# Grams as two 64-row products in two banks, a ring of three ScalarE banks, X0 by two 78-row transposes

## The reference

```python
e = stack([tbl_f[ids[:, f]] for f in range(39)], axis=1)          # 512 x 39 x 16
def _cin_layer(X0, Xi, W, b):
    Wr = W.reshape(H, F0_, Fi)
    return einsum('hjk,bjd,bkd->bhd', Wr, X0, Xi) + b[None, :, None]
Xi = X0 = e
for W, b in ((W0, b0), (W1, b1), (W2, b2)):                         # H = 128
    Xi = _cin_layer(X0, Xi, W, b); res.append(Xi.sum(axis=2))
z = concatenate(res, axis=1)                                        # 512 x 384
h = maximum(concatenate([z, dense_ctx], axis=1) @ W_top1 + b_top1, 0)
y = maximum(h @ W_top2 + b_top2, 0) @ W_top3
```

## Time and profile before

| | us |
|---|---|
| median of 3 timed runs | 656.97 (655.59 to 658.33) |
| the profiled execution | 650.86 |
| its span, first to last instruction | 649.1 |
| PE busy | 616.1 |
| DVE busy | 579.1 |
| ACT busy | 557.4 |
| POOL busy | 467.5 |

### The profile page before, as it was taken

The page is one execution under the profiler, slowest core; times in us unless marked ns, Lnnn a source line. Parts: engine busy times, 40 slices in busy tenths (PEclk is TensorE's granted clock), DMA queues, the critical chain, the costliest instruction groups (busy, mean ns, idle before and its releaser), DMA issues.

```text
span 649.1 us, 14322 instructions
## 1 busy us (share of the span) xinstructions
PE 616.1 (95%) x2591; PEld 477.4 (74%) x2591; DVE 579.1 (89%) x1230; ACT 557.4 (86%) x1763; POOL 467.5 (72%) x437
## 2 busy tenths in 40 slices
PE   0399999999999999999999999999999999999998
PEld 0167787878878787878787887878787878776573
DVE  0578999999999999999999999999999999999780
ACT  2177999999999999999999999999999999998572
POOL 6779988889797979898798979797987666220000
DMA  8543405050413223140405041322314050000100
GB/s 223 145 108 72 124 9 144 11 139 20 115 45 93 66 66 94 31 129 7 137 18 141 18 121 38 94 65 65 95 36 122 6 149 2 12 2 17 66 1 0
DMA packets 44274, 46.16 MB, mean 71 GB/s; under 512 B 20896, under 2 KB 27264, under 8 KB 44233
## 3 DMA queue, kind: packets, MB, share of 16 engines
q1 hardware_dynamic: 38626, 43.59, 23.7%
q0 software_dynamic: 5120, 1.32, 2.3%
q10 hardware_dynamic: 487, 0.74, 0.4%
HBM read 44.30 MB, written 1.31 MB: 70 GB/s over the span
## 4 chain that ended last, share of the span: by engine, by line
PE 86%; DVE 5%; DMA 3%; issue 3%; SPq 1%; DVEq 1%; ACT 1%; ACTq 0%
PE ya L513 12%; PE ya L514 12%; PE ya L515 12%; PE yd L513 9%; PE yd L515 8%; PE yd L514 8%; PE misc L496 5%; PE acc L485 4%; PE acc L484 4%; PE acc L486 3%; DVE chain L636 2%; DMA w<-in_w 2%; PE acc L489 1%; DMA tiles<-x_rows 1%; PE yd L587 1%
## 5 line engine op out<-in xcount | busy, mean ns | idle before, releaser
L764 ACT ACTIVATE prods<-ya,x0t 128x128 f32<-128x128 f32 x1472 | 453.3, 511 | 37.2 <-PE ya L515 36.5
L636 DVE SCALAR_TENSOR_TENSOR chain<-yd,x0t,chain 128x128 f32<-128x128 f32 x768 | 218.4, 343 | 1.8 <-PE yd L515 1.6
L391 POOL DMA_INDIRECT emb<-in_tables,rows x160 | 157.4, 984 | 35.6 <-issue 24.9
L513 PE MATMUL ya<-w1h,x1h 128*128 128x512 f32 (+1 forms) x384 | 166.5, 434 | 1.1 <-DVE x1l L704 1.1
L426 POOL TENSOR_TENSOR prod0l<-prod,prod0h 120x512 fp32r<-120x512 f32 x98 | 127.7, 1303 | 48.5 <-ACT prod0h L773 47.6
L514 PE MATMUL ya<-w1l,x1h 128*128 128x512 f32 (+1 forms) x384 | 147.6, 384 | 0.0
L515 PE MATMUL ya<-w1h,x1l 128*128 128x512 f32 (+1 forms) x384 | 147.4, 384 | 0.0
L305 POOL TENSOR_TENSOR prod<-tiles,x0a 120x512 f32<-120x512 f32 x105 | 137.1, 1306 | 8.6 <-DMA tiles<-x_rows 3.3
L651 DVE TENSOR_REDUCE x2t<-prods 128x128 f32<-128x1792 f32 x64 | 129.2, 2019 | 2.4 <-DVE chain L636 0.3
L651 DVE TENSOR_REDUCE prods<-prods 128x128 f32<-128x1536 f32 x64 | 111.8, 1746 | 0.0
L513 PE MATMUL yd<-w1h,x1h 128*128 128x512 f32 x256 | 102.4, 400 | 2.6 <-DVE prods L636 2.2
(11 more groups left out here) (99 smaller groups left out, 610.0 us busy)
## 6 DMA issues: line engine op xcount, KB each, us to landing
tiles<-x_rows SPq DMA_DIRECT2D x236, 78.0 KB
x0a<-x_rows SPq DMA_DIRECT2D x45, 80.0 KB
emb<-in_tables,rows POOLq DMA_INDIRECT x160
w<-in_w SPq DMA_DIRECT2D x3, 832.0 KB, 11.0
w<-in_w SPq DMA_DIRECT2D x13, 192.0 KB, 2.4
tiles<-x_rows SPq DMA_DIRECT2D x32, 42.0 KB
x<-x_rows SPq DMA_DIRECT2D x16, 78.0 KB
x<-x_rows SPq DMA_DIRECT2D x16, 77.8 KB
```

Of the source, the lines that this page charges most:

```text
L391: pool.indirect_dma_start(emb[:, c % 2, fo * D:(fo + 1) * D], None, a["tables"], bass.IndirectOffsetOnAxis(ap=rows[:, c, fo:fo + 1].bitcas ...
L513: pe.matmul(out, x1h[:, c % 2, xs], w1h[:, cols], start=True, stop=False)
L636: dve.scalar_tensor_tensor(out, product, x, run if step else b1[:, :], ALU.mult, ALU.add).then_inc(yd_used, 1)
L764: mm = act.activation(prods[:, :, slot_of(q) + i], ya[(NA * g + k) % YA][:, i * H:(i + 1) * H], ACT.Copy, scale=turned(c)[:, g * F1 + j:g ...
```

## The change

Four things change together.

1. A gram becomes two products of 64 rows. The two halves of a group's partitions now hold 4 samples each (`HB`), so the diagonal has 4 x 40 = 160 columns for both, and the mask repeats every 4 rows. Rows 0 to 63 go into bank `pair[:, 0]`, rows 64 to 127 into `pair[:, 1]`. ACT's copy reads both banks in one instruction. `misc` is the first bank of `pair`.
2. For the second bank the ring of ScalarE's banks shrinks from four to three (`YA`). In the tail the last hidden product takes `pair[:, 1]`.
3. Within a chunk all columns of the first half of the samples come before those of the second, group by group 64 and 64. So the rows in DRAM are stored as two halves of 256 columns, and each load and store addresses half rows: 1 KB pieces where there were 2 KB, and 64 bytes in the store where there were 128.
4. `x0` holds two copies (`XB = 2`), loaded by two DMAs in place of three, and two transposes of 78 rows turn it.

```diff
+HB = GB // 2
+HROWS = P // 2
+HCOLS = COLS // 2
-XB = 3
+XB = 2
-YA, YD = 4, 2
+YA, YD = 3, 2
+DIAGS = 2
-        diag = sb("diag", [P, 2, GB, F1])
+        diag = sb("diag", [P, DIAGS, HB, F1])
-        scratch = nc.dram_tensor("x0_rows", (CHUNKS, FP, COLS), F32, kind="Internal").ap()
-        acc0, misc = ps("acc0"), ps("misc")
+        scratch = nc.dram_tensor("x0_rows", (CHUNKS, 2, FP, HCOLS), F32, kind="Internal").ap()
+        acc0, pair = ps("acc0"), ps("pair", (P, 2, 512))
+        misc = pair[:, 0, :]
 def load_x0a(engine, x):
-                engine.dma_start(x0a[u * R0:(u + 1) * R0, :], chunk_rows(x)[0:R0, :]).then_inc(x0a_in, 16)
+                engine.dma_start(in_halves(x0a[u * R0:(u + 1) * R0, :]), chunk_rows(x)[0:R0]).then_inc(x0a_in, 16)
 def load_x0(x):
-                    sp.dma_start(x0[g * F:(g + 1) * F, 0:COLS - g], chunk_rows(x)[0:F, g:COLS]).then_inc(x0_in, 16)
+                    sp.dma_start(in_halves(x0[g * F:(g + 1) * F, :])[:, :, 0:HCOLS - g], chunk_rows(x)[0:F, :, g:HCOLS]).then_inc(x0_in, 16)
 def block_diagonal(c, g):
-                mask = const[:, C_MASK:C_MASK + GB].rearrange("p (b o) -> p b o", o=1)
-                pool.tensor_tensor(diag[:, n % 2, :, :], row.to_broadcast([P, GB, F1]),
-                                   mask.to_broadcast([P, GB, F1]), ALU.mult).then_inc(diag_ready, 1)
+                mask = const[:, C_MASK:C_MASK + HB].rearrange("p (b o) -> p b o", o=1)
+                pool.tensor_tensor(diag[:, n % DIAGS, :, :], row.to_broadcast([P, HB, F1]),
+                                   mask.to_broadcast([P, HB, F1]), ALU.mult).then_inc(diag_ready, 1)
 def turn_x0(c):
                 pe.transpose(misc[:, 0:XB * F], by_group[:, 0, :], const[0:XB * F, C_ID:C_ID + XB * F])
-                pe.transpose(misc[:, XB * F:GROUPS * F], by_group[0:F, XB, :], const[0:F, C_ID:C_ID + F]
+                pe.transpose(misc[:, XB * F:2 * XB * F], by_group[:, XB, :], const[0:XB * F, C_ID:C_ID + XB * F]
                              ).then_inc(x0t_done, 1)
 def gram_group(n, g):
-                pe.matmul(misc[:, 0:GB * F1], x2t[:, g % 2, :],
-                          diag[:, g % 2, :, :].rearrange("p b j -> p (b j)"),
-                          start=True, stop=True).then_inc(g_done, 1)
+                for h in range(2):
+                    half = slice(h * HROWS, (h + 1) * HROWS)
+                    mm = pe.matmul(pair[:, h, 0:HB * F1], x2t[half, g % 2, :],
+                                   diag[half, g % DIAGS, :, :].rearrange("p b j -> p (b j)"), start=True, stop=True)
+                mm.then_inc(g_done, 1)
 def evacuate_gram(n, i=0):
-                act.activation(gram[:, :, bass.ds(n * GB, GB)],
-                               misc[:, 0:GB * F1].rearrange("p (b j) -> p j b", b=GB),
+                cols = slice(i * HB * F1, (i + 1) * HB * F1)
+                act.activation(gram[:, :, bass.ds(n * GB, GB)].rearrange("p j (h b) -> p j h b", h=2),
+                               pair[:, :, cols].rearrange("p h (b j) -> p j h b", b=HB),
                                ACT.Copy).then_inc(g_ready, 1)
...
```

More of the change, by code:

```diff
@@ L54 @@
 C_MASK = 0
-C_ID = C_MASK + GB
+C_ID = C_MASK + HB
 C_ALL = C_ID + P
@@ L274, in chunk_rows, with in_halves @@
         def chunk_rows(c):
-            return scratch[bass.ds(c, 1), :, :].rearrange("c r n -> (c r) n")
+            return scratch[bass.ds(c, 1), :, :, :].rearrange("c h r n -> r (c h) n")
+        def in_halves(x):
+            return x.rearrange("p (h n) -> p h n", h=2)
         def turned(c):
@@ L293, in load_tile @@
             for row, a, b in segments(i):
-                engine.dma_start(tiles[a:b, i % L0_TILES, :],
-                                 chunk_rows(x)[row:row + b - a, :]).then_inc(tile_in[i % L0_TILES], 16)
+                engine.dma_start(in_halves(tiles[a:b, i % L0_TILES, :]),
+                                 chunk_rows(x)[row:row + b - a]).then_inc(tile_in[i % L0_TILES], 16)
         def multiply0(engine, x, i):
@@ L306, in multiply0 @@
                                  ALU.mult).then_inc(prod0_ready, 1)
-        hid, hid2 = (acc0, ya[0], ya[1], ya[2]), (yd[1], ya[3])
+        hid, hid2 = (acc0, ya[0], ya[1], ya[2]), (yd[1], pair[:, 1, :])
         block = ctx.enter_context(nc.Block())
@@ L316, in store_x0 @@
                 sp.wait_ge(x0_ready, x + 1)
[L317 to L320, removed]
+                by_row = scratch[x, :, :, :].rearrange("h (f o) n -> (h f) (o n)", f=FI)
+                for i, cols in enumerate((slice(0, FT * HCOLS), slice(FT * HCOLS, FO * HCOLS))):
+                    sp.dma_start(by_row[:, cols].rearrange("q (p b) -> p q b", b=CB // 2),
+                                 xt[0:(cols.stop - cols.start) // (CB // 2), i, :].rearrange("p (q b) -> p q b", b=CB // 2),
                                  ).then_inc(scratch_in, 16)
@@ L398, in block_diagonal @@
                 pool.wait_ge(x0t_ready, c + 1)
-                wait_done(pool, g_done, n - 1)
+                wait_done(pool, g_done, n - DIAGS + 1)
                 row = x0t[:, c % XT, g * F1:(g + 1) * F1].rearrange("p (o j) -> p o j", o=1)
-                mask = const[:, C_MASK:C_MASK + GB].rearrange("p (b o) -> p b o", o=1)
-                pool.tensor_tensor(diag[:, n % 2, :, :], row.to_broadcast([P, GB, F1]),
-                                   mask.to_broadcast([P, GB, F1]), ALU.mult).then_inc(diag_ready, 1)
+                mask = const[:, C_MASK:C_MASK + HB].rearrange("p (b o) -> p b o", o=1)
+                pool.tensor_tensor(diag[:, n % DIAGS, :, :], row.to_broadcast([P, HB, F1]),
+                                   mask.to_broadcast([P, HB, F1]), ALU.mult).then_inc(diag_ready, 1)
             def clear_dense():
@@ L664, in sum_dims @@
                     dve.wait_ge(l0_done, T0 + z_tiles)
-                dve.tensor_reduce(z[:, bass.ds(c * CB, CB)].rearrange("p (g b) -> p g b", g=GROUPS),
-                                  x1[:, :].rearrange("p (g d b) -> p g b d", g=GROUPS, d=D), AX.X,
+                dve.tensor_reduce(z[:, bass.ds(c * CB, CB)].rearrange("p (g b) -> p g b", g=2 * GROUPS),
+                                  x1[:, :].rearrange("p (g d b) -> p g b d", g=2 * GROUPS, d=D), AX.X,
                                   ALU.add).then_inc(z_sums, 1)
@@ L730, in evacuate_layout, with by_half @@
                 wait_done(act, scratch_in, 2 * 16 * c)
-                act.activation(xt[:, 0, :], misc[:, 0:P], ACT.Copy)
-                act.activation(xt[0:FO * D - P, 1, :], misc[0:FO * D - P, P:2 * P], ACT.Copy).then_inc(x0_ready, 1)
+                def by_half(x, order):
+                    return x.rearrange(f"p ({order} b) -> p f h b", h=2, b=CB // 2)
+                act.activation(by_half(xt[:, 0, :], "h f"), by_half(misc[:, 0:P], "f h"), ACT.Copy)
+                act.activation(by_half(xt[0:FO * D - P, 1, :], "h f"), by_half(misc[0:FO * D - P, P:2 * P], "f h"),
+                               ACT.Copy).then_inc(x0_ready, 1)
             def evacuate_x0t(c):
@@ L748, in evacuate_x1, with evacuate_gram @@
                                ACT.Copy).then_inc(x1h_ready, 1)
-            def evacuate_gram(n):
+            def evacuate_gram(n, i=0):
                 act.wait_ge(g_done, n + 1)
-                act.activation(gram[:, :, bass.ds(n * GB, GB)],
-                               misc[:, 0:GB * F1].rearrange("p (b j) -> p j b", b=GB),
+                cols = slice(i * HB * F1, (i + 1) * HB * F1)
+                act.activation(gram[:, :, bass.ds(n * GB, GB)].rearrange("p j (h b) -> p j h b", h=2),
+                               pair[:, :, cols].rearrange("p h (b j) -> p j h b", b=HB),
                                ACT.Copy).then_inc(g_ready, 1)
@@ L851, in constants @@
     for row in range(P):
-        pack[row, C_MASK + row % GB] = 1.0
+        pack[row, C_MASK + row % HB] = 1.0
         pack[row, C_ID + row] = 1.0
```

## The result

The changed kernel takes 661.13 us (median of 9 runs, 659.8 to 662.37), the kernel before 656.04 us beside it (9 runs, 653.18 to 659.38): ratio 1.0069, 95% interval 1.005 to 1.0087. It is slower by 0.7%, about 4.5 us by the ratio (the medians lie 5.1 us apart). The forecast was +16.2 us, 673.2 us: the right direction, more than three times the size. The time lies within the stated 658 to 686, near its lower end, and within 0.3 us of rival A's 661.4. The experiments show that A's sum is right by luck: two of its terms are wrong, and their errors cancel.

What follows compares the result with a forecast made beforehand. The prediction took PE to bound the loop, with DVE not far behind. Grams +20.1, transposes -5.1, banks +0.3 and DMA +0.9 gave +16.2 us on 656.97, so 673.2 us; range 658 to 686 for 8 in 10.

Steps and rivals of the forecast that it cites:

- rival A: Grams on PE: halves overlap fully but the emptying stays, 59 x 0.14 = +8.3 us, in all 661.4 us; chance 0.15.
- A nanosecond added to PE there is a nanosecond of the span.: Steady loop: PE, busy 36.00 of 36 us, is the bound, so time added to PE lengthens the span equally.
- Part 1, entering and leaving, 0.21 and 0.20: Each gram on PE: emptying costs 0.21 us before the 64-row passes and 0.20 us in the product behind.
- Part 1, the overlap: Four passes of a gram: half of one pass saved, 0.54 - 0.07 = 0.47 us, so +0.34 us per gram.
- The forecast's own sign of being wrong, passes that fill 0.27 us: Stated test in the profile after: prediction wrong if a gram's four passes fill 0.27 us rather than 0.47.
- Part 1, the count: 59 of 64 grams lie where PE is the bound and count in full: 59 x 0.34 = +20.1 us.
- Part 2, the transposes: X0's transposes on PE: two of 78 rows empty nothing, saving 0.34 us in 15 of 16 chunks, -5.1 us.
- DVE lets 1.2 through: Per chunk: DVE works 33.9 of 35.1 us, so a faster PE can give back at most 1.2 us.
- Part 3, three banks: ScalarE's ring cut from four banks to three: 0.35 us to spare at the tightest place, +0.3 us over the run.
- Part 4, DMA: Half-length rows: covered in the loop; more pieces in chunk 0's loads and store cost +0.9 us.
- Rivals B, C and D: In order: no emptying, 653.1 us, chance 0.16; emptying also between halves, 689.1, 0.10; ring or DMA binds, about 680, 0.09.

Runs made afterwards that it cites:

- the same-rows kernel: The changed kernel with both halves of each gram multiplied on rows 0 to 63, leaving out half the contraction; ratio 1.024 to the kernel before, period 36.19 us.

## Why the prediction was wrong

- **"A nanosecond added to PE there is a nanosecond of the span."** This is the step at which the mechanism failed. It was read from 36.00 busy of 36. A product that waits counts as busy, so PE's wait of 0.27 us per chunk for DVE's bank did not show, though the chain shows it as 0.50 us for one product. Each chunk has a quarter that DVE sets. The forecast named DVE only as a floor for the whole chunk (33.9 of 35.1 us) and for the last chunk. This step made two errors, in the count of grams and in the worth of the transposes, that nearly cancel (+2.7 to 3.7 us and -4.4 us).
- **Part 1, entering and leaving, 0.21 and 0.20.** Right. The 39-row transposes foretold it: entering 0.33 us to the end of the first pass, less its 0.135, is 0.20, and the product behind takes 0.42 to 0.43 instead of 0.23.
- **Part 1, the overlap.** Mis-sized, and this is the term that put the number off: 0.07 us taken, 0.27 measured, so +0.13 per gram and not +0.34. 59 x 0.21 = 12.4 us, where forecast and measurement differ by 11.7. The forecast's own sign of being wrong, passes that fill 0.27 us, came true. I argued from program order and from loads 0.11 us apart; four loads took 0.30 us in all, their starts in two pairs 7 ns apart. On the same rows no two loads start closer than 0.11 us, so a pair must be one load of each half. The Trainium skill ("TensorE: Matmul & The Clock Gate", Part 3, Packing small matmuls), set beside the sum, was the better guide: with the same-rows kernel (0.94 against 0.67) a run here now shows the like for two 64-row halves.
- **Part 1, the count.** 59 grams at full price was wrong. Per chunk 0.04 + 0.12 + 0.12 + 0 counts: the gram done in group 0 replaces some 0.09 us that it already waited for DVE's sum (0.64 us in the chain for 0.54, with the 64-row grams undone), the one in group 3 lies in DVE's quarter. For all grams that is 4 us by the loop, 5.0 by the ratios.
- **Part 2, the transposes.** Cost right (0.31 of 0.34 us saved each), worth wrong: -5.1 us forecast, ratio 0.9989 measured, 0.7 us. "DVE lets 1.2 through" overlooked where the saving lies.
- **Part 3, three banks.** Right within its size: ratio 1.0006. In the loop of the changed kernel PE waits for ACT 0.6 us, three times.
- **Part 4, DMA.** Right as to the loop: 64,282 packets for 38,626 on the main queue, its share 23.0% for 23.7%. At the start the tile transfers show 4.18 us for 4.25 in the chain. The 0.9 us is not visible: with half rows and three banks the ratio is 0.9993, with the transposes alone 0.9989, 0.3 us apart and within the noise.
- **Rivals B, C and D** are out. The first load of a gram does wait (0.35 us), the gram's 0.47 us has no room for an emptying between the halves, and neither three banks nor half rows cost anything that is seen.
- **Rival A** gave 8.3 - 5.1 + 1.2 = +4.4 us and +4.5 was measured: grams taken too dear by 3.3 to 4.3 us, and the transposes' saving too large by 4.4 us. The agreement is no proof of its working.

## What to carry to other kernels

Before pricing an edit, find where each engine waits for the other within one turn of the loop, by the starts of one engine's first instruction per group and by products that stand in the chain with more than their usual time; only an edit in a stretch that its own engine sets counts, and busy time of 100% doesn't say that. A product on few rows between products on many costs PE an emptying before and one behind, so halving a 0.54 us product into overlapping halves lost: 0.40 us for the two emptyings, 0.27 saved. By this estimate such products pay only in longer runs of the same kind, which no run here tried. Undo one part at a time even where the total fits: here it fitted a wrong account.

## What the runs showed of the hardware

- Products with a 64-row contraction on different row halves, in different banks, ran wholly side by side, the weight loads too (pairs 7 ns apart); on the same rows not at all (0.94 against 0.67 us per gram).
- Going from 128 rows to 64 and back cost 0.20 us each time, the same as with 39 rows; 78, 80, 117 and 120 rows cost nothing of the kind (0.04 us behind the 78-row transposes at most).
- DMA pieces of 1 KB in place of 2 KB cost nothing measurable here: with 2.9% fewer bytes the queue's share of time went from 23.7% to 23.0%, though it moved two thirds more packets.
- The first chunk had standstills of 4.0 to 8.4 us in six of seventeen profiles, in five of them with the clock at 1.2 GHz for some us behind, on some chips and not on others; the profile doesn't name the cause, and no run here was made for it.
